# One branch over the general path, and layer two's first adjacency pieces loaded inside layer one

## The chip, the cores and the metric

The kernel runs on one core of one Trainium2 chip. The metric is the device time of one execution in microseconds (us); before the change the median of three runs is 2069.12 us.

## What is computed

Two graph convolutions on 6,250 nodes of 256 numbers, then a feed-forward layer that sends every node to two of eight experts:

```python
x = x + gnn(layernorm(x))      # two layers: relu(A_norm @ (h @ W) + b)
x = x + ffn(layernorm(x))      # top 2 of 8 experts, gelu(x @ W1 + b1) @ W2 + b2

def _gcn_conv(x, W, b, src, dst, n):
    h = x @ W
    deg = segment_sum(1, dst_with_loops);  dinv = rsqrt(deg)
    msgs = h[src] * (dinv[src] * dinv[dst])[:, None]
    return segment_sum(msgs, dst, num_segments=n) + b
```

There are 206,250 edges, sorted by destination. The lines of the two convolutions are shortened here; the layer norm has no weights of its own in front of the graph layers.

## The kernel before, in words

Nodes stand in 49 blocks of 128. The adjacency is held as counts: for a block of 128 destinations a tile `[128, 49 * 128]` of fp16 says how many edges lead from every source to every destination. A block's sum is then 49 matmuls of 128 x 512 (the node rows are kept as a high and a low fp16 half, hence 512 columns). For 40 of the 49 blocks the sums are made so ("dense"); for the other nine, source rows are gathered from DRAM ("takes", an indirect DMA on GpSimd, POOL, each followed by one matmul with a one-hot), 311 takes in a layer.

The program is a row of blocks (`nc.Block`), one after the other. In a block each of the five engines (TensorE PE, VectorE DVE, ScalarE ACT, GpSimd POOL, SyncE SP) has its own straight list of instructions; engines wait for each other by semaphores. At the end of a block all engines meet at a barrier, POOL clears the block's semaphores (L168) and all meet again (L169).

- **Layer one** (`build_layer_one`) builds the counts from one-hots `oh_lane` and `oh_cell` (VectorE, L802) by matmuls of one-hots (L954), empties them from PSUM (ScalarE, L1055), adds the self loops, sums (L925), takes (L567, L938) and writes to DRAM: each dense block's counts to `adj` for layer two (SP, L511), and each block's finished rows to `rows_d[1]` (SP, L514). A counter `n` over 512 banks and some steps after them sets the order of everything. At its end SP waits for the stores of the counts.
- **The general path** follows: four program blocks, `build_general_tables`, `build_general_rows`, `build_general_adjacency` and `build_general_layer`. They redo layer one for inputs that don't fit its tables. Whether the input fits stands in one word `fits`, set in layer one (L725). Each engine reads it once into a register (L305), and in each of the four blocks every engine compares it (`choose`, L307) and jumps over its own part. On this input all of them are jumped over. In the adjacency block a small index table (L1420, L1422, L1440) is computed in either case.
- **Layer two** (`build_layer_two`) reads `adj` back in half blocks ("pieces", 800 and 768 KB) into a ring of three (`ADJ_RING`), issued by SP (L1841), and sums again (L1871), with takes (L1798, L1887). A sum of a block is cut in five parts; part by part a slot counter orders what each engine does. Behind each sum follow the turn-over (`turn_over`), the product with the layer's weights `w` (`product`, L1905), and the rest on VectorE and ScalarE. SP first loads `w` and `b` (L1820, L1821), then three pieces, two blocks of `x` and small tables. PE and VectorE wait for `w` and `b` (`w_in`) before they begin. POOL writes rows of zeros to DRAM (L1768, L1769), starts a weight load, and takes from then on.
- **Routing and experts** come after it and are not touched.

All SBUF tiles have addresses: `rows[1]` is at the top of SBUF (`k.top`), the rest is allocated from below.

Of the kernel before, what the change touches and what calls it, by code (L numbers as in the profile page):

```python
# [193 lines left out]
def build_constants(k):  # L194

    nc = k.nc
    k.ident = k.sb("ident", [P, P], fp32)
    k.ones = k.sb("ones", [P, P], fp32)
    k.held_pool = k.sb("held_pool", [1, POOL_HOLDS + 1], fp32)
    k.held_act = k.sb("held_act", [P, 1], fp32)  # L200
    k.self_loop = k.sb("self_loop", [P, P], fp16)
    k.held_dve = k.sb("held_dve", [1, 1], fp32)
    k.eps = k.sb("eps", [P, 1], fp32)
    k.tri = k.sb("tri", [P, P], fp32)
# [12 lines left out]
    k.value_base = k.sb("value_base", [P, VALUES, TOKEN_TILES], fp32)  # L217
    k.pad_value = k.sb("pad_value", [P, 1], fp32)
    k.gb = k.sb("gb", [P, 2, EXPERTS * KF], fp32)
    k.b1 = k.sb("b1", [P, EXPERTS * HB], fp32)  # L220
    k.slot_gate = k.sb("slot_gate", [P, TOKEN_TILES], fp32)
    k.slot_token = k.sb("slot_token", [P, TOKEN_TILES], i32)
    k.pair_expert = k.sb("pair_expert", [1, 2 + PAIRS], i32)
    k.take_src = k.sb("take_src", [P, len(TAKES)], i32)
    k.take_lane = k.sb("take_lane", [P, len(TAKES), 2], bf16)
    k.ident_h = k.sb("ident_h", [P, P], fp16)
    k.rows_d = [k.dr(f"rows_d{n}", [PAD_NODES, 2 * D], fp16) for n in range(2)]
    k.rows1_out = k.nc.alloc_semaphore("rows1_out")
    k.adj = k.dr("adj", [BLOCKS, P, BLOCKS * P], fp16)
# [18 lines left out]
PLACE = {b: i for i, b in enumerate(ENDED)}  # L248

# [65 lines left out]
def build_layer_one(k, gst):  # L315
# [13 lines left out]
    k.fits = own("fits", [1, 1], u16)  # L329
# [3 lines left out]
    with ExitStack() as st:  # L333
# [57 lines left out]
        oh_lane = sb("m_oh_lane", [P, SLOTS_R, P], fp16)  # L391
        oh_cell = sb("m_oh_cell", [P, SLOTS_R, CELLS2], fp16)
# [21 lines left out]
        assert nc.sbuf_base <= k.top, nc.sbuf_base - k.top  # L414
# [69 lines left out]
        def _(sp):  # L484
# [597 lines left out]
def build_general_tables(k, gst):  # L1082
# [9 lines left out]
    with ExitStack() as st:  # L1092
# [50 lines left out]
        def _(sp):  # L1143
# [12 lines left out]
            choose(k, nc.sync, apart=apart)  # L1156

        @block.vector
        def _(dve):
# [107 lines left out]
            choose(k, nc.vector, apart=apart)  # L1267

        @block.scalar
        def _(act):  # L1270
# [17 lines left out]
            choose(k, nc.scalar, apart=apart)  # L1288

        @block.gpsimd  # L1290
        def _(pool):
# [16 lines left out]
            choose(k, nc.gpsimd, apart=apart)  # L1308

        @block.tensor  # L1310
        def _(pe):
# [27 lines left out]
            choose(k, nc.tensor, apart=apart)  # L1339


def build_general_rows(k):
# [3 lines left out]
    with ExitStack() as st:  # L1346
# [7 lines left out]
        @block.sync  # L1354
        def _(sp):
            def apart():
                sp.dma_start(xs[:], k.io["x"].rearrange("(b p) d -> p b d", p=P)).then_inc(x_in, 16)
            choose(k, nc.sync, apart=apart)

        @block.vector  # L1360
        def _(dve):
# [21 lines left out]
            choose(k, nc.vector, apart=apart)  # L1383

        @block.scalar
        def _(act):
            def apart():
                act.wait_ge(var_ready, BLOCKS)
                nc.scalar.activation(rstd[:], mv[:, :, 1], ACT.Sqrt, bias=k.eps[:]).then_inc(root, 1)
            choose(k, nc.scalar, apart=apart)  # L1390


def build_general_adjacency(k):
# [7 lines left out]
    with ExitStack() as st:  # L1401
# [17 lines left out]
        def _(pool):  # L1419
# [15 lines left out]
            choose(k, nc.gpsimd, apart=apart)  # L1435

        @block.vector
        def _(dve):
# [21 lines left out]
            choose(k, nc.vector, apart=apart)  # L1460

        @block.tensor
        def _(pe):
# [21 lines left out]
            choose(k, nc.tensor, apart=apart)  # L1485

        @block.scalar
        def _(act):
# [29 lines left out]
            choose(k, nc.scalar, apart=apart)  # L1518

        @block.sync  # L1520
        def _(sp):
# [8 lines left out]
            choose(k, nc.sync, apart=apart)  # L1530


def build_general_layer(k):
# [9 lines left out]
    with ExitStack() as st:  # L1543
# [20 lines left out]
        def _(sp):  # L1564
# [8 lines left out]
            choose(k, nc.sync, apart=body)  # L1573

        @block.tensor
        def _(pe):
# [38 lines left out]
            choose(k, nc.tensor, apart=body)  # L1615

        @block.scalar
        def _(act):
# [12 lines left out]
            choose(k, nc.scalar, apart=body)  # L1631

        @block.vector
        def _(dve):
# [24 lines left out]
            choose(k, nc.vector, apart=body)  # L1659


def build_layer_two(k):
# [4 lines left out]
    with ExitStack() as st:  # L1667
# [7 lines left out]
        adj = sb("_adj", [P, ADJ_RING, ADJ_HALF * P], fp16)  # L1675
# [29 lines left out]
        assert nc.sbuf_base <= k.top, nc.sbuf_base - k.top  # L1705
# [14 lines left out]
        adj_in = [sem(f"_adj_in{q}") for q in range(ADJ_RING)]  # L1720
# [98 lines left out]
        def _(sp):  # L1819
# [13 lines left out]
            def load_adj(o, m):  # L1833

                b, a = m // 2, m % 2 * ADJ_HALF
                n = min(ADJ_HALF, BLOCKS - a)
# [4 lines left out]
                sp.dma_start(adj[:, m % ADJ_RING, 0:n * P], k.adj[b][:, a * P:(a + n) * P]).then_inc(adj_in[m % ADJ_RING], 16)  # L1841

            def program(o):
# [9 lines left out]
                for slot in range(o.end):  # L1853
                    for m in range(2 * o.dense):
                        if slot == max(PARTS * (m - ADJ_RING + 1) // 2, 0):
                            load_adj(o, m)
# [6 lines left out]
        def _(pe):  # L1863
# [66 lines left out]
            pe.wait_ge(w_in, WEIGHTS)  # L1930
# [57 lines left out]
        def _(dve):  # L1988
# [112 lines left out]
            def program(o):  # L2101
# [44 lines left out]
            dve.wait_ge(w_in, WEIGHTS)  # L2146
# [469 lines left out]
```

## Time and profile before

| what | us |
|---|---|
| median of three runs | 2069.12 |
| fastest and slowest run | 2066.21, 2073.44 |
| span of the profiled execution (its own time from first to last instruction) | 2052.8 |
| what lies around the span, by the median | 16.3 |
| PE busy, share of the span | 1871.5, 91% |
| VectorE, GpSimd, ScalarE busy | 1351.6, 1143.9, 733.3 |

The page also cuts the span into 40 slices of 51.3 us; in tenths, PE's busy share and its granted clock are

```profile
PE   5789999999999975999999999944999999999997
PEclk9999999999999997999999999975999999999998
```

The profiled execution has no time of its own beside the span; the three runs were timed without a profile. Times in the rows below are counted from the start of the span. An engine's sequencer work (branches, barriers, loads of registers, issues of DMAs) is not counted as busy; in rows its engine has a "q" at the end, and PE's stands under "PEldq". "[9.60 <-X]" behind a row is the idle time of the engine before it and what ended it.

### The profile page before, as it was taken

To read this page: it belongs to the slowest core of one execution; us is meant where nothing else is said; L and a number is where in the kernel's file an instruction comes from. 1 tells how busy PE (TensorE), PEld (TensorE's weight loads), DVE (VectorE), ACT (ScalarE), POOL (GpSimd) and SP (SyncE) were. 2 spreads that over 40 slices of the span, in tenths; PEclk is the share of its full clock that TensorE was granted. 3 is DMA by queue.
4 is the path that set the end of the run, shared out by engine and by line. 5 is a ranking of instruction groups with operands and counts; after the bars stand their busy time and mean duration, and the time that the engine had idled before them with its cause. 6 is when DMAs were issued, how large, how long until landed. Compare 5 with 4: busy or idle time off the path is not lost. (4 is left out here: it accounts for less than half of the span.)

```text
span 2052.8 us, 40739 instructions
## 1 busy us (share of the span) xinstructions
PE 1871.5 (91%) x13425; PEld 1223.2 (60%) x13426; DVE 1351.6 (66%) x3358; ACT 733.3 (36%) x1669; POOL 1143.9 (56%) x1210
## 2 busy tenths in 40 slices
PE   5789999999999975999999999944999999999997
PEld 4545555554555532544544444423989989989996
DVE  7866766676667642566675757567676676666664
ACT  5744544444444420111111111112444444444442
POOL 6236666666666614667666666302455655555553
PEclk9999999999999997999999999975999999999998
DMA  9464555554455536787877788824233332333322
GB/s 292 121 217 167 180 191 173 174 181 167 170 181 174 177 121 215 242 278 259 266 249 270 268 303 269 283 83 193 42 50 52 49 49 47 49 49 49 50 44 27
DMA packets 126419, 329.51 MB, mean 161 GB/s; under 512 B 20736, under 2 KB 80000, under 8 KB 119360
## 3 DMA queue, kind: packets, MB, share of 16 engines
q0 software_dynamic: 59072, 142.05, 26.3%
q1 hardware_dynamic: 47376, 167.36, 22.7%
q10 hardware_dynamic: 19824, 18.23, 2.8%
q8 instruction: 82, 1.34, 0.3%
q14 instruction: 65, 0.53, 0.1%
HBM read 214.10 MB, written 113.45 MB: 160 GB/s over the span
## 5 line engine op out<-in xcount | busy, mean ns | idle before, releaser
L925 PE MATMUL mp_o<-rows,m_counts 128*128 128x512 f16 x1960 | 491.0, 382 | 8.5 <-ACT m_counts L1055 8.5
L1871 PE MATMUL rp_o<-rows,r_adj 128*128 128x512 f16 x1960 | 460.2, 382 | 31.3 <-DMA r_adj<-adj 31.3
L567 POOL DMA_INDIRECT m_x_t<-rows_d,take_src x311 | 368.2, 1184 | 202.6 <-PE mp_x L938 162.8
L1798 POOL DMA_INDIRECT r_took<-rows_d,take_src x311 | 323.7, 1041 | 186.4 <-PE rp_g L1887 122.1
L1055 ACT ACTIVATE m_counts<-mp 128x490 f16<-128x490 f32 (+4 forms) x544 | 292.2, 558 | 352.4 <-PE mp L954 346.0
L1871 PEld LDWEIGHTS rp_o<-rows,r_adj 128*128 128x128 f16 x1960 | 192.8, 98 | 251.0 <-DMA r_adj<-adj 31.8
L2427 PE MATMUL fp_h<-f_xt,w 128*128 128x256 f16 x2688 | 304.8, 274 | 0.3 <-DVE f_xt L2523 0.3
L2446 PE MATMUL fp_y<-w,f_hh 128*128 x2688 | 302.4, 273 | 0.0
L925 PEld LDWEIGHTS mp_o<-rows,m_counts 128*128 128x128 f16 x1960 | 183.0, 98 | 185.1 <-issue 11.5
L2427 PEld LDWEIGHTS fp_h<-f_xt,w 128*128 x2688 | 264.0, 98 | 31.7 <-issue 0.7
L2446 PEld LDWEIGHTS fp_y<-w,f_hh 128*128 128x128 f16 x2688 | 263.0, 98 | 30.4
L954 PEld LDWEIGHTS mp<-m_oh_cell,m_oh_lane 128*128 128x128 f16 x2560 | 163.8, 98 | 140.6 <-DVE m_oh_lane L802 24.8
L954 PE MATMUL mp<-m_oh_cell,m_oh_lane 128*128 128x98 f16 x2560 | 194.2, 208 | 29.7 <-DVE m_oh_lane L802 14.5
L2499 ACT ACTIVATE f_h<-fp_h,b 128x256 f32<-128x256 f32 x448 | 188.4, 475 | 76.1 <-PE fp_h L2427 71.4
L802 DVE TENSOR_TENSOR m_oh_lane<-lane_b,m_edge_lane 128x1920 f16<-128x1920 bf16 x171 | 201.8, 1180 | 8.9 <-PE mp L954 8.7
L2363 POOL DMA_INDIRECT out_dram<-f_weighted,f_to x112 | 184.8, 1650 | 30.4 <-issue 29.5
L180 POOL TENSOR_TENSOR held_pool<-held_pool 1x1 f32<-1x1 f32 x204 | 68.7, 339 | 210.7 <-DMA out_dram<-f_weighted,f_to 165.9
L2556 DVE TENSOR_TENSOR f_hh<-f_h,f_hh 128x512 f16<-128x512 f32 x224 | 156.1, 697 | 7.7
L802 DVE TENSOR_TENSOR m_oh_cell<-m_cells,m_edge_cell 128x1470 f16<-128x1470 bf16 x171 | 159.2, 931 | 0.0
L783 DVE TENSOR_TENSOR m_take_oh<-lane_b,take_lane 128x640 f16<-128x640 bf16 (+1 forms) x63 | 31.2, 496 | 191.4 <-PE mp_x L938 191.4
L2351 POOL DMA_INDIRECT f_xg<-xn_rows,f_stage x112 | 115.0, 1027 | 33.9 <-issue 33.4
L2532 DVE SCALAR_TENSOR_TENSOR f_y<-fp_y,b 128x256 f32<-128x256 f32 x112 | 47.4, 424 | 121.5 <-PE fp_y L2446 120.1
(260 smaller groups left out, 1877.2 us busy)
## 6 DMA issues: line engine op xcount, KB each, us to landing
adj<-m_counts SPq DMA_DIRECT2D x40, 1568.0 KB, 5.9
r_adj<-adj SPq DMA_DIRECT2D x40, 800.0 KB, 5.2
r_adj<-adj SPq DMA_DIRECT2D x40, 768.0 KB, 5.2
r_raw<-in_L_ffn_W_dram POOLq DMA_DIRECT2D x16, 1024.0 KB, 8.4
w_parts<-r_parts POOLq DMA_DIRECT2D x8, 1024.0 KB, 6.7
w<-w_parts SPq DMA_DIRECT2D x4, 2048.0 KB
rows<-in_x_dram SPq DMA_DIRECT2D x7, 896.0 KB, 20.1
rows_d<-rows SPq DMA_DIRECT2D x7, 896.0 KB, 4.6
```

Source lines behind the costliest of these rows:

```text
L567: pool.indirect_dma_start(out=took[:, r, :], out_offset=None, in_=k.rows_d[0], in_offset=bass.IndirectOffsetOnAxis(ap=k.take_src[:, i:i + ...
L802: nc.vector.tensor_tensor(out[:, r:r + items].rearrange("p r (v t) -> p r v t", t=2), bc(row[:].rearrange("p (v t) -> p v t", t=2)[:, None ...
L925: mm = nc.tensor.matmul(ps_o[q], counts[:, q, s, :], k.rows[0][:, s, :], start=i == 0, stop=i == BLOCKS - 1)
L954: mm = nc.tensor.matmul(bank(n)[:, i * CELLS2:(i + 1) * CELLS2], oh_lane[:, slot(n) + i, :], oh_cell[:, slot(n) + i, :], start=True, stop= ...
L1055: last = nc.scalar.activation(counts[:, q, :, lo - b * P:hi - b * P].rearrange("p h (a d) -> p h a d", d=STEP), items[:, :, (lo - first_ds ...
L1798: pool.indirect_dma_start(out=took[:, r, :], out_offset=None, in_=k.rows_d[1], in_offset=bass.IndirectOffsetOnAxis(ap=k.take_src[:, i:i + ...
L1871: mm = nc.tensor.matmul(ps_o[b % 2], adj[:, m % ADJ_RING, at:at + P], rows[:, s, :], start=s == 0, stop=s == BLOCKS - 1)
L2363: pool.indirect_dma_start(out=k.io["out"], out_offset=bass.IndirectOffsetOnAxis(ap=to[:, i:i + 1], axis=0), in_=weighted[:, i % YR, :], in ...
L2427: mm = nc.tensor.matmul(ps_h[b][:, j * PAIR:(j + 1) * PAIR], w, xt[:, q, xh, c, :], start=i == 0, stop=i == 5)
L2446: mm = nc.tensor.matmul(ps_y[s][:], hh[:, q, xh, h, s * P:(s + 1) * P], w, start=i == 0, stop=i == 3 * HB - 1)
L2499: g = nc.scalar.activation(h32[:, h, :], ps_h[b][:, j * PAIR:(j + 1) * PAIR], ACT.Gelu, bias=k.b1[:, bass.ds(ex[m + 1] * HB + h, 1)], scal ...
L2556: nc.vector.tensor_tensor(hh[:, q, 1, part], h32[:, part], hh[:, q, 0, part], ALU.subtract).then_inc(h_lo, 1)
```

## The change

Two edits, and what they need.

1. The four blocks of the general path are put under one branch: after layer one every engine loads the word `fits` again and compares it once (`nc.If`); the `choose` in each of the blocks goes. The word moves to the constants, so that it stays.
2. SP loads the first three adjacency pieces of layer two in layer one, at step 512, once the last bank of counts is made. The ring is a fixed piece of SBUF at the upper end of the one-hots `oh_lane` and `oh_cell`, which nobody reads after the last bank; their address is fixed for it. The semaphores of the ring, `adj_in`, live through both layers. Layer two's SP leaves out these three loads (`next_adj`). PE waits for `w_in` ahead of its first product, and VectorE ahead of its first `activate`, no longer at the beginning.

```diff
+    k.adj_in = [k.nc.alloc_semaphore(f"adj_in{q}") for q in range(ADJ_RING)]
+    k.oh_at = (k.top - SLOTS_R * (P + CELLS2) * 2) // 64 * 64
+    k.ring_at = (k.top - ADJ_RING * ADJ_HALF * P * 2) // 64 * 64
+    k.adj_ring = nc.alloc_sbuf_tensor_at("adj_ring", [P, ADJ_RING, ADJ_HALF * P], fp16, offset=k.ring_at)
...
+def load_adj(k, eng, m):
+
+    b, a = m // 2, m % 2 * ADJ_HALF
+    n = min(ADJ_HALF, BLOCKS - a)
+    eng.dma_start(k.adj_ring[:, m % ADJ_RING, 0:n * P], k.adj[b][:, a * P:(a + n) * P]).then_inc(k.adj_in[m % ADJ_RING], 16)
...
-        oh_lane = sb("m_oh_lane", [P, SLOTS_R, P], fp16)
-        oh_cell = sb("m_oh_cell", [P, SLOTS_R, CELLS2], fp16)
+        oh_lane = nc.alloc_sbuf_tensor_at("m_oh_lane", [P, SLOTS_R, P], fp16, offset=k.oh_at)
+        oh_cell = nc.alloc_sbuf_tensor_at("m_oh_cell", [P, SLOTS_R, CELLS2], fp16, offset=k.oh_at + SLOTS_R * P * 2)
...
                             sp.dma_start(k.adj[b], counts[:, b % 2].rearrange("p h d -> p (h d)")).then_inc(stored[b % 2], 16)
+                    if n == BANKS_D:
+
+                        sp.wait_ge(bank_done, BANKS_D)
+                        sp.wait_ge(stored[0], 16)
+                        sp.wait_ge(stored[1], 16)
+                        for m in range(ADJ_RING):
+                            load_adj(k, sp, m)
...
-            choose(k, nc.sync, apart=apart)
+            apart()
...
+                if m < ADJ_RING and o.takes:
+                    return
...
                 pe.wait_ge(agg_copied, b + 1)
                 if b:
                     pe.wait_ge(pre_ready, b)
+                else:
+                    pe.wait_ge(w_in, WEIGHTS)
...
-            pe.wait_ge(w_in, WEIGHTS)
             choose_order(nc.tensor, program)
...
                     q = i % 2
+                    if i == 0:
+                        dve.wait_ge(w_in, WEIGHTS)
...
-            dve.wait_ge(w_in, WEIGHTS)
             choose_order(nc.vector, program)
...
-            with ExitStack() as ust:
-                build_general_tables(k, ust)
-                build_general_rows(k)
-                build_general_adjacency(k)
-            build_general_layer(k)
+            flag = nc.alloc_registers("fits_all")
+            nc.regs_load(flag, k.fits[0:1, 0:1])
+            with nc.If(nc.snap(flag, min_val=0, max_val=1) < 1):
+                with ExitStack() as ust:
+                    build_general_tables(k, ust)
+                    build_general_rows(k)
+                    build_general_adjacency(k)
+                build_general_layer(k)
```

Where `choose` went, the same change stands fourteen more times; it is shown once. How the instructions of an engine's list move is shown at three places. A name in brackets is the semaphore an instruction waits for; semaphores are used again, so a wait of layer two stands under the name that its number had first in layer one. `rows_49` and `rows_50` are `rows[1]`.

**PE, from the last sum of layer one to the end of the first jump.** Before (the last two rows belong to the first of the four blocks, whose entry is the row with the barrier):

```order
L925 MATMUL mp_o<-rows,m_counts 128x512 [waits m_emptied,m_agg]
L925 MATMUL mp_o<-rows,m_counts 128x512 x47
L925 MATMUL mp_o<-rows,m_counts 128x512 [waits m_looped]
L307 UNCONDITIONAL_BRANCH
L1310 UNCONDITIONAL_BRANCH [waits barrier_Pool_Activation_PE_DVE_SP_release]
L307 COMPARE_AND_BRANCH
L307 UNCONDITIONAL_BRANCH
```

Now:

```order
L943 MATMUL mp_o<-rows,m_counts 128x512 [waits m_emptied,m_agg]
L943 MATMUL mp_o<-rows,m_counts 128x512 x47
L943 MATMUL mp_o<-rows,m_counts 128x512 [waits m_looped]
L319 UNCONDITIONAL_BRANCH
L2592 TENSOR_LOAD fits [waits barrier_Pool_Activation_PE_DVE_SP_release]
L1775 COMPARE_AND_BRANCH
L1328 UNCONDITIONAL_BRANCH
```

The wait for the barrier has the flag's load behind it in place of the entry to the first block, and one comparison; the rows of the blocks that follow have no comparison of their own.

**PE, the beginning of layer two.** `m_io` is the wait for `w` and `b`; `m_hi`, `m_lo` and `m_cells` are the three pieces. Before:

```order
L1602 MATMUL sp_h<-s_w,s_agg_t 128x256
L310 UNCONDITIONAL_BRANCH
L1862 UNCONDITIONAL_BRANCH [waits barrier_Pool_Activation_PE_DVE_SP_release]
L307 COMPARE_AND_BRANCH [waits m_io]
L1871 MATMUL rp_o<-rows_49,r_adj 128x512 [waits m_hi]
L1871 MATMUL rp_o<-rows_49,r_adj 128x512 x24
L1871 MATMUL rp_o<-rows_49,r_adj 128x512 [waits m_lo]
L1871 MATMUL rp_o<-rows_49,r_adj 128x512 x23
```

Now:

```order
L1775 UNCONDITIONAL_BRANCH [waits barrier_Pool_Activation_PE_DVE_SP_release]
L1880 UNCONDITIONAL_BRANCH
L319 COMPARE_AND_BRANCH
L1889 MATMUL rp_o<-rows_50,adj_ring 128x512 [waits adj_in0]
L1889 MATMUL rp_o<-rows_50,adj_ring 128x512 x24
L1889 MATMUL rp_o<-rows_50,adj_ring 128x512 [waits adj_in1]
L1889 MATMUL rp_o<-rows_50,adj_ring 128x512 x23
L1889 MATMUL rp_o<-rows_50,adj_ring 128x512 [waits adj_in2]
```

The comparison no longer waits for the weights, and the pieces' semaphores are those that layer one's SP raises; the wait `m_io` stands at the first `rp_h<-r_w,r_agg_t`, behind the first takes.

**SP, the end of layer one.** `m_lo2` is a finished row block. Before:

```order
L511 DMA adj<-m_counts 128x6272 [waits m_looped]
L514 DMA rows_d<-rows_49 128x512 [waits m_lo2]
L511 DMA adj<-m_counts 128x6272 [waits m_looped] x2
L514 DMA rows_d<-rows_49 128x512 [waits m_lo2] x5
L307 UNCONDITIONAL_BRANCH [waits m_rows0_out,m_stored1,m_stored0]
L1142 UNCONDITIONAL_BRANCH [waits barrier_Pool_Activation_PE_DVE_SP_release]
L307 COMPARE_AND_BRANCH
```

Now:

```order
L532 DMA rows_d<-rows_50 128x512 [waits m_lo2]
L522 DMA adj<-m_counts 128x6272 [waits m_looped] x2
L260 DMA adj_ring<-adj 128x3200 [waits m_stored1,m_stored0,m_bank]
L260 DMA adj_ring<-adj 128x3072
L260 DMA adj_ring<-adj 128x3200
L532 DMA rows_d<-rows_50 128x512 [waits m_lo2] x5
L319 UNCONDITIONAL_BRANCH [waits m_rows0_out,m_stored1,m_stored0]
L2592 TENSOR_LOAD fits [waits barrier_Pool_Activation_PE_DVE_SP_release]
L1775 COMPARE_AND_BRANCH
```

Three loads of pieces stand between the last two stores of counts and the last five writes of rows; the three `r_adj<-adj` in front of `r_x<-in_x_dram` in layer two are gone from SP's list.

## Rows read from the trace of the kernel before

**Rows 1.** The page, part 1, whole span: busy us, share, instructions.

```profile
PE 1871.5 (91%) x13425; PEld 1223.2 (60%) x13426; DVE 1351.6 (66%) x3358; ACT 733.3 (36%) x1669; POOL 1143.9 (56%) x1210
```

**Rows 2.** Page, part 5: group, count | busy us, mean ns | idle before.

```profile
L1871 PE MATMUL rp_o<-rows,r_adj 128*128 128x512 f16 x1960 | 460.2, 382 | 31.3 <-DMA r_adj<-adj 31.3
```

**Rows 3.** Timeline, 735 to 800 us: start, duration, what [idle before].

```profile
748.53 10.74 PE L925 MATMUL mp_o<-rows,m_counts 128*128 128x512 f16 x49 [0.76 <-ACT m_counts L1055]
749.30 12.65 SPq L514 DMA_DIRECT2D rows_d<-rows  x5
760.62 0.99 DVE L762 TENSOR_TENSOR rows<-m_act_in,rows 128x256 f16<-128x256 f32 x2
781.81 0.40 SPq L1820 DMA_DIRECT2D r_w<-in_L_gnn_W_dram  x1
783.34 1.33 SPq L1841 DMA_DIRECT2D r_adj<-adj  x3
790.62 9.75 PE L1871 MATMUL rp_o<-rows,r_adj 128*128 128x512 f16 x33 [31.34 <-DMA r_adj<-adj]
```

**Rows 4.** PE's release from a block's barrier (L169), first and fifth.

```profile
L169 PEldq EVENT_SEMAPHORE  x1: 51/51/51, 763.4 to 763.4; - x1
...
L169 PEldq EVENT_SEMAPHORE  x1: 51/51/51, 781.7 to 781.7; - x1
```

**Rows 5.** PE's branches (L307) in three blocks: min/median/max ns, starts.

```profile
L307 PEldq COMPARE_BRANCH  x2: 73/1737/3401, 763.6 to 763.7; - x2
...
L307 PEldq COMPARE_BRANCH  x2: 71/1920/3770, 772.0 to 772.1; - x2
...
L307 PEldq COMPARE_BRANCH  x2: 77/1918/3758, 776.9 to 777.0; - x2
```

**Rows 6.** PE in layer one: flag's load (L305), branch falling through (L307).

```profile
L305 PEldq TENSOR_LOAD <-fits x1: 479/479/479, 75.6 to 75.6; - x1
...
L307 PEldq COMPARE_BRANCH  x1: 88/88/88, 76.2 to 76.2; - x1
```

**Rows 7.** First and fourth block: branches, and the first instruction (DRAIN) behind.

```profile
L307 POOLq COMPARE_BRANCH  x2: 39/40/41, 763.5 to 763.5; - x2
...
L1092 POOLq DRAIN  x1: 115/115/115, 764.0 to 764.0; - x1
...
L307 DVEq COMPARE_BRANCH  x2: 43/45/47, 776.8 to 776.9; - x2
...
L1543 DVEq DRAIN  x1: 59/59/59, 781.0 to 781.0; - x1
```

**Rows 8.** Stretches: us, busy us of five engines, clock, DMA share, GB/s.

```profile
749.00:755.00 6.00, 6.00 (x29) 2.71 (x28) 0.71 (x3) 0.42 (x1) 0.00 (x0) 1.00 0.84 333
763.00:782.00 19.00, 0.00 (x0) 0.00 (x0) 0.70 (x3) 0.00 (x0) 1.18 (x3) 0.50 0.04 11
...
761.50:790.60 29.10, 0.00 (x0) 0.00 (x0) 2.69 (x11) 0.00 (x0) 3.91 (x10) 0.50 0.27 88
790.60:795.60 5.00, 4.99 (x12) 1.79 (x13) 0.00 (x0) 0.00 (x0) 2.82 (x3) 0.50 1.02 416
795.60:800.60 5.00, 5.00 (x24) 2.25 (x23) 0.00 (x0) 0.00 (x0) 3.79 (x5) 1.00 1.04 378
```

**Rows 9.** DMA issues: KB each, us to landing; one load, 40 stores (L511).

```profile
r_b<-in_L_gnn_b_dram SPq DMA_DIRECT2D x1, 128.0 KB, 6.4
...
adj<-m_counts SPq DMA_DIRECT2D x40, 1568.0 KB, 5.9
```

**Rows 10.** Layer two's first takes: issue, PE's use (timeline), landing (DMA list).

```profile
792.17 1.04 POOL L1798 DMA_INDIRECT r_took<-rows_d,take_src  x1 [7.44 <-DMA xn_rows<-r_took]
...
805.60 0.59 PE L1887 MATMUL rp_g<-r_took,r_take_oh 128*128 128x512 f16 x2
...
r_took<-rows_d,take_src POOLq DMA_INDIRECT x8, 6.4
```

**Rows 11.** Waits of POOL, 790 to 1360 us: total us, times, longest.

```profile
POOL r_took L1798 <- PE rp_g L1887: 122.1, 130, 4.3
```

More of the change, by code:

```diff
@@ L203, in build_constants @@
     k.eps = k.sb("eps", [P, 1], fp32)
+    k.fits = k.sb("fits", [1, 1], u16)
     k.tri = k.sb("tri", [P, P], fp32)
@@ L328, in build_layer_one @@
     own = lambda name, shape, dt: gst.enter_context(nc.sbuf_tensor(name, shape, dt))
-    k.fits = own("fits", [1, 1], u16)
     k.fits_flag = {}
@@ L413, in build_layer_one @@
         took = x_t[:].rearrange("p r c n -> p (r c n)").bitcast(fp16).rearrange("p (r d) -> p r d", r=TAKE_RING)
-        assert nc.sbuf_base <= k.top, nc.sbuf_base - k.top
+        assert nc.sbuf_base <= k.oh_at, nc.sbuf_base - k.oh_at
         ps = st.enter_context(nc.psum_tensor("mp", [P, BANKS * BANK], fp32))
@@ L1266, in apart @@
                 nc.vector.memset(k.edge_cell[:, ITEMS:], -1.0)
-            choose(k, nc.vector, apart=apart)
+            apart()
         @block.scalar
@@ L1287, in apart @@
                 nc.scalar.activation(tot[:], tmp[:], ACT.Sqrt).then_inc(root_done, 1)
-            choose(k, nc.scalar, apart=apart)
+            apart()
         @block.gpsimd
@@ L1307, in apart @@
                             in_offset=bass.IndirectOffsetOnAxis(ap=tile_i[:, c:c + 1], axis=0)).then_inc(got[c % 4], 16)
-            choose(k, nc.gpsimd, apart=apart)
+            apart()
         @block.tensor
@@ L1338, in apart @@
                         nc.tensor.transpose(ps_t[(2 * c + j) % 4][:], rows[:, c % 4, :], k.ident[:]).then_inc(t_done, 1)
-            choose(k, nc.tensor, apart=apart)
+            apart()
 def build_general_rows(k):
@@ L1357, in apart @@
                 sp.dma_start(xs[:], k.io["x"].rearrange("(b p) d -> p b d", p=P)).then_inc(x_in, 16)
-            choose(k, nc.sync, apart=apart)
+            apart()
         @block.vector
@@ L1382, in apart @@
                     link(nc.vector.tensor_tensor(lo, xs[:, b, :], hi, ALU.subtract))
-            choose(k, nc.vector, apart=apart)
+            apart()
         @block.scalar
@@ L1389, in apart @@
                 nc.scalar.activation(rstd[:], mv[:, :, 1], ACT.Sqrt, bias=k.eps[:]).then_inc(root, 1)
-            choose(k, nc.scalar, apart=apart)
+            apart()
 def build_general_adjacency(k):
@@ L1434, in apart @@
                 in_pairs(nc.gpsimd, BLOCKS, loop)
-            choose(k, nc.gpsimd, apart=apart)
+            apart()
         @block.vector
@@ L1459, in apart @@
                 in_pairs(nc.vector, BLOCKS, one_hots)
-            choose(k, nc.vector, apart=apart)
+            apart()
         @block.tensor
@@ L1484, in apart @@
                 in_pairs(nc.tensor, BLOCKS, items)
-            choose(k, nc.tensor, apart=apart)
+            apart()
         @block.scalar
@@ L1517, in apart @@
                 in_pairs(nc.scalar, BLOCKS, empty)
-            choose(k, nc.scalar, apart=apart)
+            apart()
         @block.sync
@@ L1529, in apart @@
                     sp.wait_ge(stored[q], 16 * ((BLOCKS + 1 - q) // 2))
-            choose(k, nc.sync, apart=apart)
+            apart()
 def build_general_layer(k):
@@ L1572, in body @@
                     sp.dma_start(adj[:, q, :], k.adj[b]).then_inc(adj_in[q], 16)
-            choose(k, nc.sync, apart=body)
+            body()
         @block.tensor
@@ L1614, in body @@
                             product(b - 1)
-            choose(k, nc.tensor, apart=body)
+            body()
         @block.scalar
@@ L1630, in body @@
                     nc.scalar.activation(k.rows[1][:, b, 0:D], pre[:, q, :], ACT.Copy).then_inc(hi_done, 1)
-            choose(k, nc.scalar, apart=body)
+            body()
         @block.vector
@@ L1658, in body @@
                                             ALU.subtract).then_inc(lo_done, 1)
-            choose(k, nc.vector, apart=body)
+            body()
 def build_layer_two(k):
@@ L1674, in build_layer_two @@
         brow = sb("_b", [P, D], fp32)
-        adj = sb("_adj", [P, ADJ_RING, ADJ_HALF * P], fp16)
+        adj = k.adj_ring
         took = sb("_took", [P, TAKE_RING, 2 * D], fp16)
@@ L1704, in build_layer_two @@
         dense = sb("_dense", [P, BLOCKS, EXPERTS], fp32)
-        assert nc.sbuf_base <= k.top, nc.sbuf_base - k.top
+        assert nc.sbuf_base <= k.ring_at, nc.sbuf_base - k.ring_at
         ps_o = [pb(f"p_o{i}", [P, 2 * D], fp32) for i in range(2)]
@@ L1719, in build_layer_two @@
                                     "gates_out"))
-        adj_in = [sem(f"_adj_in{q}") for q in range(ADJ_RING)]
+        adj_in = k.adj_in
         took_in = [sem(f"_took_in{r}") for r in range(TAKE_RING)]
@@ L1831, in small, with next_adj @@
                 sp.dma_start(b1_rows, k.io["L0_ffn_b1"].rearrange("e (c p) -> (e c) p", p=P)).then_inc(small_in, 16)
-            def load_adj(o, m):
-                b, a = m // 2, m % 2 * ADJ_HALF
-                n = min(ADJ_HALF, BLOCKS - a)
+            def next_adj(o, m):
+                if m < ADJ_RING and o.takes:
+                    return
                 if m >= ADJ_RING and (m - ADJ_RING) % 2 == 0:
@@ L1840, in load_adj @@
                     sp.wait_ge(summed, o.place[(m - ADJ_RING) // 2] + 1)
-                sp.dma_start(adj[:, m % ADJ_RING, 0:n * P], k.adj[b][:, a * P:(a + n) * P]).then_inc(adj_in[m % ADJ_RING], 16)
+                load_adj(k, sp, m)
             def program(o):
@@ L1855, in program @@
                         if slot == max(PARTS * (m - ADJ_RING + 1) // 2, 0):
-                            load_adj(o, m)
+                            next_adj(o, m)
                     for i in range(BLOCKS):
```

## The prediction

> **What bounds the kernel now.** I read the page's engine shares first: TensorE (PE) is busy for 91% of the span [rows 1], so time is won mostly where it stands still. The costliest groups of instructions come next. The 1,960 adjacency matmuls of layer two (L1871) have 31.3 us of idle time in front of them, all of it put down to the load `r_adj<-adj`, and none besides [rows 2]: inside layer two the sums run back to back. The timeline shows the stop itself: the last matmul of layer one ends at 748.53 + 10.74 = 759.3 us, the first of layer two starts at 790.6 [rows 3]. The page's releaser names only the wait that ended last, so I split the stop. From 759.3 to 763.4 layer one ends: VectorE finishes the last row block (760.62 + 0.99 = 761.6), SP issues its write (749.30 + 12.65 = 761.95), then the barriers at the end of the block [rows 3, 4]. From 763.4 to 781.7, 18.3 us, five engines pass four program blocks of the general path, in which on this input nothing but an index table is computed [rows 4]. From 781.7 to 790.6, 8.9 us, PE waits for its first loads: they are issued at 781.81 (weights) and 783.34 (adjacency), and the matmul starts at 790.62 [rows 3].
>
> Why are empty blocks dear? The branch rows answer. PE's second branch in three of the blocks lasts 3.40, 3.77 and 3.76 us, although a branch that just falls through lasts 0.09 [rows 5, 6]; so I read a jump over a long skipped body as a wait for the code at its target. VectorE shows the same as a late arrival: branch at 776.9, next instruction at 781.0. POOL, whose skipped body in the first block is short, arrives at 764.0 after a branch at 763.5 [rows 7]. Every block then adds its barriers, and its slowest jump is paid again.
>
> **The change, part by part.**
>
> *One branch for four blocks.* The barrier release at 763.4 stays. What follows is one load of the flag, one comparison and one jump. Load to branch takes 0.6 us on PE where layer one does the same (75.6 to 76.2) [rows 6]. The new jump, over all the bodies at once, is not in the trace. Nearest rows: PE's three jumps, 3.40 to 3.77 [rows 5], and VectorE's 4.1 [rows 7]. Lower end: no wait at all, 0.1, if the target happened to be there. Upper end: two such waits in a row, 4.1 + 3.8 = 7.9, if the first piece of code ends soon after the target or the five engines' fetches hinder each other. I take 3.8, PE's own dearer row. PE then stands at layer two's first branch at 763.4 + 0.1 + 0.6 + 3.8 = 767.9, instead of 781.7.
>
> *The first three pieces loaded ahead.* SP now issues them behind the 40th adjacency store and ahead of the last five row writes: three issues, 1.33 us [rows 3]. Three of the row writes are ready at once and go 1.3 us later, nobody being in need of them; the last are ready only near 761, so SP has the time. Bytes: store 1,568 KB, pieces 800 + 768 + 800 KB, three row writes of 128 KB, 4.4 MB. The engines moved 333 GB/s in 749 to 755 and 416 GB/s when the same pieces were loaded in layer two [rows 8], so the burst that begins at 748.9 is over between 759.5 and 762.2. The pieces are there 6 us before PE wants them. Layer one's end waits for the 40th store: by the median of all 40 it lands 5.9 us after its issue [rows 9], at 754.8, and even last in the burst by 762.2 against an end at 762.0. I take 0; the ends are 0 and 0.2.
>
> *Waits for the weights moved to the first product.* PE no longer waits for `w` and `b` ahead of the sums, VectorE not ahead of its first one-hots. `r_b` lands 6.4 us after its issue [rows 9]; with SP in layer two by 768.3 at the latest and 1.4 us for both issues that is 776.1 at the latest. PE's first product stands behind the first take, 805.60 - 790.62 = 15.0 us after the start [rows 3, 10], so at 783 or later. Nothing waits; if the cover were gone, PE would stand with the sums queued behind it.
>
> With both gone PE starts about 0.3 us (my choice; a branch of 0.09 and the first issue) after it arrives, at 768.2: **22.4 us earlier** than 790.6. Ends of the unknown jump: 764.5 (26.1 earlier) and 772.3 (18.3 earlier).
>
> *What is late next.* POOL's first take. Before, it is issued at 792.17, 10.5 us after POOL entered layer two, of which 7.44 are a wait for a zero row to land among the adjacency loads; takes then land after 6.4 us [rows 10]. If POOL enters no earlier than PE (767.9) and nothing gets quicker, take 0 lands at 784.8, and PE wants it at 768.2 + 15.0 = 783.2: a stall of 1.6. If POOL arrives early, as its short jump lets me expect, or the zero row no longer shares the engines with 2.4 MB of pieces, none. I take 0.
>
> *Clock.* PE's granted clock is 0.50 from 761.5 to 795.6, the lower level (1.2 GHz), though PE worked until 759.3; the first 12 matmuls of layer two take 5.0 us, the next 24 as long at 1.00 [rows 8]. Restarting at 768.2 still comes after a stop of 8.9 us, so I count the same slow start on both sides: 0. Ends: 2.5 us won if the clock is up (12 matmuls at full rate), 2.5 lost if the low stretch doubles.
>
> *Nothing for the rest.* One-hots and tiles at other addresses, the flag among the constants, semaphores held outside the blocks: the same instructions with the same shapes, no row shows a price, and I bound it by 0 on both sides. The rest of the program starts 22.4 us earlier and runs as before: in layer two POOL waits for PE 130 times, 122.1 us in all [rows 11], so PE sets that stage and the shift is carried through.
>
> Sum: span 2052.8 - 22.4 = 2030.4. What lies around the span is 2069.12 - 2052.8 = 16.3 us by the median of the runs, and stays. **2046.7 us**, 1.1% below that median.
>
> **Rivals.**
>
> *A. The jump is dearer.* Five engines fetch at once, and the transfers that fetch code may meet data. For it: three of four blocks show 3.4 us or more with few engines fetching; these fetches ran while the engines moved 11 GB/s [rows 8], the kindest case. Against it: by my burst the ring is in by 762.2. Price: about one more wait, 3.8: 2050.5 us. The Trainium skill, "DMA: Bandwidth & Descriptors", section "Issuing engines are not separate DMA queues", says that transfers issued by any engine run on the same 16 DMA engines and interleave; it speaks against loads placed shortly before a jump. The trace has no jump beside a busy queue, so it neither confirms nor denies it for code.
>
> *B. The takes gate the start.* The stall of 1.6 above, up to 4 with slower landings: 2048.3 to 2050.7. For: two transfers stand between POOL's entry and PE's need. Against: fewer bytes at that moment.
>
> *C. The other way: slower.* The code of layer two no longer arrives in time. Before, the engines stood 8.9 us at its door after their jump, time for later code to be brought in; now they run on at once, and PE could wait again and again along its stream. Place: gaps between L1871's successors with no releaser. Price 3.4 to 3.8 each; from seven of them on (7 x 3.4 = 23.8) the change loses, and ten cost 38 - 22.4 = 15.6: 2084.7 us. Against: nothing but the load wait stands before those 1,960 matmuls now [rows 2], so the stream keeps up once it runs.
>
> *D. Hardly anything changes.* The burst delays the store on which layer one's end waits, or the branch isn't reached earlier, so that 16 of the 22 us go. It would need the store at 778, against the 762.2 of the worst sharing: 2063 to 2069 us.
>
> *E. A cheaper start.* The jump finds its target, or the clock is up: 2041 to 2044.5 us.
>
> **How the numbers follow.** Forecast 0.62, A 0.17, B 0.08, E 0.07, C 0.03, D 0.03. About 0.3%, 6.2 us, can be told from no change, as the runs of before spread from 2066.21 to 2073.44. Forecast, A, B and E are all faster by more: 0.94; D is the same: 0.03; C slower: 0.03. The range takes in A with its upper end (2050.8) and E (2041), widened by some 3 us at the top and 1 at the bottom for that spread: 2040 to 2054.
>
> **What would show it.** Right: PE's idle time in front of the first adjacency matmul of layer two near 9 us instead of 31.3; one branch row of 3.4 to 4 us on PE near 764; no releaser `adj_ring<-adj` for that wait; the three loads issued near 750 and landed by 762; the distance from that matmul to the end as before. Wrong in the jump: the branch row at 7 us, or a gap without a releaser soon after the start. Wrong in the takes: PE waiting for `r_took` some 15 us after its start. Wrong altogether: layer one ending later than 763.4, or idle time spread along layer two.

## The result, and the profile after

The change takes 2046.77 us, the median of four runs (2043.71 to 2052.19); before takes 2069.31, the median of four (2066.21 to 2073.44). The ratio is 0.988 with a 95% interval of 0.9861 to 0.9899: faster by 1.2% (the medians alone differ by 22.5 us, 1.1%). The forecast was 2046.7.

The profiled execution of the change has a span of 2045.8 us and a time of 2047.49. Its page has this for the costliest matmuls of layer two (columns as in [rows 2]):

```profile
L1889 PE MATMUL rp_o<-rows,adj_ring 128*128 128x512 f16 x1960 | 455.9, 380 | 8.9 <-issue 8.9
```

31.3 us of idle time have become 8.9, and the releaser is no load any more. The timeline of 760 to 802 us shows the boundary (columns as in [rows 3]):

```profile
766.41 10.74 PE L943 MATMUL mp_o<-rows,m_counts 128*128 128x512 f16 x49 [0.76 <-ACT m_counts L1073]
...
767.27 2.59 SPq L260 DMA_DIRECT2D adj_ring<-adj  x3
769.90 9.94 SPq L532 DMA_DIRECT2D rows_d<-rows  x5
...
778.50 0.99 DVE L780 TENSOR_TENSOR rows<-m_act_in,rows 128x256 f16<-128x256 f32 x2
...
782.22 0.39 SPq L1838 DMA_DIRECT2D r_w<-in_L_gnn_W_dram  x1
...
786.04 14.06 PE L1889 MATMUL rp_o<-rows,adj_ring 128*128 128x512 f16 x58 [8.89 <-issue]
...
788.00 1.04 POOL L1816 DMA_INDIRECT r_took<-rows_d,take_src  x1 [3.05 <-DMA xn_rows<-r_took]
...
799.93 0.59 PE L1905 MATMUL rp_g<-r_took,r_take_oh 128*128 128x512 f16 x2
```

Layer one's last matmul ends at 766.41 + 10.74 = 777.15 us, layer two's first starts at 786.04. SP issues the three pieces at 767.27, right at the start of that last block of matmuls, as forecast. The take that PE needs first is issued at 788.00 and used at 799.93; POOL waits 3.05 us for its zero row, where it waited 7.44 [rows 10], and PE has no idle time at 799.93. What is left of the stop shows in the sequencers' rows (columns as in [rows 4]):

```profile
L169 PEldq EVENT_SEMAPHORE  x1: 51/51/51, 781.3 to 781.3; - x1
...
L2592 PEldq TENSOR_LOAD <-fits x1: 298/298/298, 781.5 to 781.5; - x1
...
L1775 SPq COMPARE_BRANCH  x1: 50/50/50, 781.7 to 781.7; - x1
...
L1775 PEldq COMPARE_BRANCH  x1: 3912/3912/3912, 781.9 to 781.9; - x1
```

The barrier lets PE go at 781.3, as long after the last matmul (4.2 us) as before (4.1). Load and comparison of the flag take 0.6 us to 781.9, the one jump 3.91, and 0.2 us later PE is at work. SP's branch lasts 0.05 us: its next instruction, the load of the weights, goes at 782.22, beside PE's jump. The windows (columns as in [rows 8]) show the burst of the ring, and the clock at the restart:

```profile
766.80:780.80 14.00, 10.35 (x48) 4.49 (x46) 2.88 (x8) 0.91 (x3) 0.00 (x0) 1.00 0.92 335
781.00:782.00 1.00, 0.00 (x0) 0.00 (x0) 0.00 (x0) 0.00 (x0) 0.00 (x0) 1.00 0.00 0
782.00:788.80 6.80, 2.76 (x7) 1.04 (x8) 1.74 (x9) 0.00 (x0) 3.50 (x9) 0.50 0.71 188
788.80:793.80 5.00, 5.00 (x24) 2.25 (x23) 0.00 (x0) 0.00 (x0) 3.79 (x5) 1.00 0.99 356
```

The burst from 766.8 runs for 14.0 us at 335 GB/s and is over just before the jump: from 781 to 782 us nothing moves. The granted clock is still 1.00 in that row; it is 0.50, the lower level of 1.2 GHz, from 782.0 to 788.8 only, and 1.00 behind it; before it was 0.50 from 761.5 to 795.6 [rows 8].

**A surprise in the sum.** The two profiled spans, 2052.8 and 2045.8 us, differ by 7.0 us, the medians by 22.5. The rest lies at the beginning. In the stretch from 34 to 56 us the first profile of before has (same columns)

```profile
34.00:56.00 22.00, 17.98 (x88) 13.62 (x87) 20.13 (x50) 13.45 (x37) 16.22 (x16) 0.92 1.04 334
```

and the profile of the change

```profile
34.00:56.00 22.00, 5.95 (x14) 3.72 (x15) 10.16 (x22) 1.54 (x4) 14.43 (x14) 0.59 0.86 264
```

so PE is busy there for a third of the time it was (14 matmuls recorded, against 88), and everything behind is some 18 us late: the last block of layer one starts at 766.41 where it started at 748.53 [rows 3]. The first experiment asks whose delay that is.

### The profile page after: what moved, and what is told of

It reads as the page before. It is cut to its first block and busy times, and to the rows that moved or that the text cites. A ratio compares the mean times of both kernels' runs of the same rounds, so it can differ in the third digit from the quotient of the medians.

```text
span 2045.8 us, 40624 instructions
## 1 busy us (share of the span) xinstructions
PE 1867.4 (91%) x13425; PEld 1222.5 (60%) x13426; DVE 1345.9 (66%) x3357; ACT 729.1 (36%) x1669; POOL 1146.3 (56%) x1208
## 5 line engine op out<-in xcount | busy, mean ns | idle before, releaser
L1889 PE MATMUL rp_o<-rows,adj_ring 128*128 128x512 f16 x1960 | 455.9, 380 | 8.9 <-issue 8.9
L1889 PEld LDWEIGHTS rp_o<-rows,adj_ring 128*128 128x128 f16 x1960 | 191.9, 98 | 225.9 <-issue 11.2
L2383 POOL DMA_INDIRECT out_dram<-f_weighted,f_to x112 | 190.2, 1699 | 30.2 <-issue 29.1
L2519 ACT ACTIVATE f_h<-fp_h,b 128x256 f32<-128x256 f32 x448 | 183.2, 481 | 66.1 <-PE fp_h L2447 62.3
L2495 ACT ACTIVATE held_act<-ones 128x1 f32<-128x1 f32 x56 | 11.4, 203 | 316.2 <-PE fp_x L2431 301.8
```

The costliest lines, as they stand in the source:

```text
L1889: mm = nc.tensor.matmul(ps_o[b % 2], adj[:, m % ADJ_RING, at:at + P], rows[:, s, :], start=s == 0, stop=s == BLOCKS - 1)
L2383: pool.indirect_dma_start(out=k.io["out"], out_offset=bass.IndirectOffsetOnAxis(ap=to[:, i:i + 1], axis=0), in_=weighted[:, i % YR, :], in ...
L2519: g = nc.scalar.activation(h32[:, h, :], ps_h[b][:, j * PAIR:(j + 1) * PAIR], ACT.Gelu, bias=k.b1[:, bass.ds(ex[m + 1] * HB + h, 1)], scal ...
```

## The experiments

"Stop" is the idle time that the timeline gives in front of layer two's first adjacency matmul.

| run | stop, us | PE's jump, us | median of runs, us |
|---|---|---|---|
| before, first profile | 31.34 | 3.40, 3.77, 3.76 | 2069.31 |
| before again | 32.03 | 3.76, 4.03, 3.84 | 2068.78 |
| branch only | 16.09 | 4.21 | 2052.23 |
| loads only | 22.16 | 3.42, 3.27, 3.46 | 2062.06 |
| weights waited for at the front | 9.82 | 3.91 | 2047.13 |
| the change | 8.89 | 3.91 | 2046.77 |
| one more block | 13.92 | 3.31, 4.49 | 2054.39 |
| three pieces by the jump | 12.97 | 6.68 | 2049.44 |
| two pieces by the jump | 11.42 | 5.63 | 2049.28 |
| one piece by the jump | 9.16 | 3.84 | 2047.55 |
| x loaded one piece after the other | 8.49 | 3.52 | 2046.32 |

Runs of one kernel spread over up to 14 us, so a few us are read from the stop, not from the median.

### Before, once more

No edit.

> The kernel before, unchanged. Question: the profiled execution of before has a span of 2052.8 us, 16.3 below the median of its timed runs, while every run of the change lies only 1.7 us above its own span; and the first 100 us of the change's profile are some 18 us longer than those of before's. Theory (a lucky profile): the first profile of before caught an execution with a quick beginning; typical runs of before begin as slowly as the change does. Then the span here is 1.7 us below the time, 2064 to 2071, the last matmul block of layer one starts near 766 (748.5 in the first profile), and the stop from its end to the first adjacency matmul of layer two is again 31 us. Rival (the change slows the beginning): the span is again near 2053 beside a time of 2054.5 to 2069, layer one's last block starts near 749, and the moved tiles or the constants cost the change 18 us at its beginning that some other gain pays for.

Measured: 2068.78 us, ratio to before 0.9998 (0.9984 to 1.0012), span 2067.1, 1.7 below that execution's time of 2068.78. Its window from 34 to 56 us is that of the change:

```profile
34.00:56.00 22.00, 5.70 (x13) 3.52 (x14) 13.50 (x34) 1.92 (x5) 13.54 (x14) 0.60 0.85 272
```

The flag that ends the tables of layer one is loaded by PE at 75.6 us in the first profile of before [rows 6], here (same columns) at

```profile
L305 PEldq TENSOR_LOAD <-fits x1: 476/476/476, 93.5 to 93.5; - x1
```

and in the change at

```profile
L317 PEldq TENSOR_LOAD <-fits x1: 474/474/474, 94.1 to 94.1; - x1
```

The stop is what it was:

```profile
808.93 6.29 PE L1871 MATMUL rp_o<-rows,r_adj 128*128 128x512 f16 x19 [32.03 <-DMA r_adj<-adj]
```

So the first profile of before shows an untypically quick execution, and the slow beginning is no cost of the change. Of the 51 times of before in all the comparisons made here, none is below 2064 us. The two profiles of before also differ in how much they recorded: the first holds 26,872 updates of semaphores, the second 17,664. Whether the first execution was quick by chance, or because it was recorded in another way, no run shows.

### The branch alone

```diff
-                    if n == BANKS_D:
-                        sp.wait_ge(bank_done, BANKS_D)
...
-                            load_adj(k, sp, m)
...
-                if m < ADJ_RING and o.takes:
-                    return
...
+            pe.wait_ge(w_in, WEIGHTS)
             choose_order(nc.tensor, program)
...
+            dve.wait_ge(w_in, WEIGHTS)
             choose_order(nc.vector, program)
```

> The change without its loads: one branch over the general path, but the three pieces are loaded at the front of layer two and PE and VectorE wait for the weights there, as before. Theory (jump and loads overlap): SP's jump is short, so its loads go out some 2.4 us after the barrier release and land 7.3 us later, beside PE's jump; PE starts 4.9 us later than with the whole change, the stop is 9.3 + 4.9 = 14.2 us, the gain 31.3 - 14.2 = 17.1: 2052.2 us. Rival (additive, as the prediction summed): the gain is 18.3 - 4.5 = 13.8 and the load wait of 8.9 stays whole behind the jump: stop 17.5, 2055.5 us. Rival (the branch does nothing by itself): 2069 us.

Measured: 2052.23 us, ratio 0.9923 (0.9902 to 0.9944). PE's jump (columns as in [rows 5]), and the timeline:

```profile
L1768 PEldq COMPARE_BRANCH  x1: 4213/4213/4213, 778.6 to 778.6; - x1
```

```profile
780.20 2.52 SPq L260 DMA_DIRECT2D adj_ring<-adj  x3
...
789.88 14.28 PE L1880 MATMUL rp_o<-rows,adj_ring 128*128 128x512 f16 x58 [16.09 <-DMA adj_ring<-adj]
```

SP's loads go out at 780.20, while PE jumps from 778.6 to 782.8, so part of their time is covered. But the first piece comes 9.7 us after its issue, where it took 7.3 before (783.34 to 790.62 [rows 3]). Why it took longer is not shown. The stop of 16.09 stands between the two theories (14.2 and 17.5): some of the load wait is covered, but less than the first had it. The median agrees with the first (2052.2), yet the interval of the ratio takes in both, so the time alone could not have told them apart. The rival that the branch does nothing by itself is out.

### The loads alone

Each of the four blocks has its own comparisons again, in place of the one branch:

```diff
-            apart()
+            choose(k, nc.tensor, apart=apart)
```

> The change without its branch: the four blocks each keep their own comparison, the pieces are loaded inside layer one and the waits for the weights stand at the first product. Theory: the 18.3 us from the barrier to layer two's branch stay, only the 8.9 us of load wait go down to about 0.3: stop 22.7 us, gain 8.6, 2060.7 us. By both theories of overlap the same here; with the branch alone at 17.1 the two gains add to 25.7 against 22.4 for both, 3.3 us counted twice; with 13.8 they add to 22.4. Rival (the code of layer two must be fetched after the jump, so part of the load wait was never the loads'): PE waits 3 to 4 us without a releaser where the loads stood, gain 5, 2064 us.

Measured: 2062.06 us, ratio 0.9957 (0.9941 to 0.9974).

```profile
800.82 14.17 PE L1889 MATMUL rp_o<-rows,adj_ring 128*128 128x512 f16 x58 [22.16 <-PEq L169]
```

The stop falls by 9.2 us against the first profile and 9.9 against the second: the load wait goes whole, and no wait for code stands where it was. PE's release from the last barrier is at 800.5, its first matmul at 800.82. That rival is out. Branch (15.3 to 15.9 us) and loads (9.2 to 9.9) add to 24.4 to 25.8, both together bring 22.5 to 23.1: some 2 to 3 us are in both, the part of the loads that lies beside the jump.

### The waits for the weights at the front

```diff
-                else:
-                    pe.wait_ge(w_in, WEIGHTS)
...
+            pe.wait_ge(w_in, WEIGHTS)
             choose_order(nc.tensor, program)
```

and the same on VectorE.

> The change with the waits for the weights back at the front of layer two, on PE and VectorE; branch and loads as in the change. Theory: SP issues the weights 0.9 us after the barrier release, the bias 0.7 later lands after 6.4 us, so PE may start 8.0 us after the release, against 4.7 in the change: stop 12.6 us, 3.3 us later than the change, 2050.1 us. Rival (the weights land in time behind the jump): 2046.8, stop 9.3. Rival (the moved waits matter more, since VectorE's one-hots for the takes are late as well): PE also stands ahead of its first take, 2052 us or more.

Measured: 2047.13 us, ratio 0.9898 (0.9871 to 0.9925).

```profile
786.87 14.00 PE L1889 MATMUL rp_o<-rows,adj_ring 128*128 128x512 f16 x58 [9.82 <-DMA r_b<-in_L_gnn_b_dram]
```

My 3.3 us were too many: the bias, issued at 782.56, is there when PE's wait ends at 786.7, 4.2 us after the issue and not 6.4 [rows 9]. No pieces are loaded beside it now, which may be the reason; no run tests it. The wait that was moved costs 0.9 us where it stood, too little to see in the time. The rival by which it costs nothing comes nearest.

### One more block

The last block of the general path stands outside the branch again, with comparisons of its own:

```diff
-                build_general_layer(k)
+            build_general_layer(k)
```

> The change with the last of the four blocks of the general path taken out from under the branch again: it keeps its own comparisons, its jump over its body and its barriers. Everything else as in the change. Theory (each block costs a jump and its barriers, whatever stands before it): in the profile of before that block takes 4.9 us from release to release, so the stop grows from 9.3 to 14.2 us and the time from 2046.8 to 2051.7 us; PE shows two long branches, each 3.3 to 4.2 us. Rival (a second jump is cheap, since the first has already brought code in): only the barriers, about 1.1 us, come on top: stop 10.4, 2047.9 us. Rival (the time of a jump grows with the code jumped over): the first is shorter and the second also, the two together about 3.9 plus 1.1: 2047.9 us as well, but with two branch rows of about 2 us each.

Measured: 2054.39 us, ratio 0.9928 (0.9907 to 0.995). PE's two jumps, and the stop:

```profile
L1581 PEldq COMPARE_BRANCH  x1: 3313/3313/3313, 781.5 to 781.5; - x1
...
L319 PEldq COMPARE_BRANCH  x2: 73/2280/4488, 784.9 to 785.1; - x2
```

```profile
790.70 15.21 PE L1889 MATMUL rp_o<-rows,adj_ring 128*128 128x512 f16 x58 [13.92 <-PEq L169]
```

The stop grows by 5.0 us, as the first theory has it (4.9). A second jump is not cheaper for the first, and neither is shorter for having less to skip: 3.31 us over three blocks, 4.49 over one. The median is 2.7 us above the expected 2051.7 and all four runs lie above it; the four runs of the change alone spread over 8.5 us, so these 2.7 us stay unsettled.

### The loads beside the jump

```diff
-                    if n == BANKS_D:
...
-                            load_adj(k, sp, m)
...
                 sp.wait_ge(rows0_out, 16 * X_LOADS)
+                for m in range(ADJ_RING):
+                    load_adj(k, sp, m)
```

> The change with the three loads of pieces moved from behind the last bank of counts to the very end of SP's list of layer one, behind its last waits, so that 2.4 MB are in flight while PE jumps. Theory (data hardly hurts a jump; the late loads hurt by themselves): SP's three issues delay the end of layer one by about 1.3 us; PE's jump stays at 3.9 to 4.2; the first piece lands some 8.5 us after its issue at 780.0, so PE restarts near 788.5 instead of 786.0: 2049.3 us. Rival A of the prediction (code and data share the 16 engines, so the jump takes one wait more): branch row of 7 us or more, PE restarts near 790 or later: 2051 us or more. Rival (place of the loads doesn't matter, as they land beside barrier and jump): 2046.8 to 2048 us.

Measured: 2049.44 us, ratio 0.9895 (0.9872 to 0.9918). The time is the theory's; the way to it is nearly rival A's. Jump and timeline:

```profile
L1770 PEldq COMPARE_BRANCH  x1: 6676/6676/6676, 783.8 to 783.8; - x1
```

```profile
780.52 1.31 SPq L260 DMA_DIRECT2D adj_ring<-adj  x3
...
790.67 14.06 PE L1884 MATMUL rp_o<-rows,adj_ring 128*128 128x512 f16 x58 [12.97 <-issue]
```

The jump takes 6.68 us. The list of the DMA queues (packets, MB, share of the engines) says why. First 784 to 787 us, then 787 to 788:

```profile
q1 hardware_dynamic: 226, 1.21, 101.3%
...
q1 hardware_dynamic: 46, 0.29, 105.7%
q14 instruction: 4, 0.03, 10.2%
q8 instruction: 1, 0.02, 8.1%
```

For three microseconds behind the branch the 16 engines are full with data and no packet of instructions moves; then four packets of one queue and one of the other come, and PE goes on. In the change four such packets move at once, from 782 to 783 us:

```profile
q14 instruction: 4, 0.03, 11.8%
```

Two more runs vary what is in flight.

### One and two pieces beside the jump

```diff
-                        for m in range(ADJ_RING):
+                        for m in (0, 1):
                             load_adj(k, sp, m)
...
                 sp.wait_ge(rows0_out, 16 * X_LOADS)
+                for m in (2,):
+                    load_adj(k, sp, m)
```

and `(0,)` with `(1, 2)`.

> As the run with the loads beside the jump, but only the third piece (800 KB, wanted 21 us after the restart) is issued at the end of SP's list; the first two stay where the change has them. With three pieces there PE's jump lasted 6.68 us instead of 3.91, and the code it waits for began to move only at 787.1, when the data ahead of it had drained. Theory (code waits behind the data that is in flight, in proportion to its bytes): the barrier comes 0.4 us later, 0.8 MB drain in 2.3 us and are gone before the jump's fetch: branch row 3.9 to 4.3 us, stop 9.7 to 10.2, 2047.4 us. Rival (any large transfer begun near the jump costs it a whole second wait): 6.5 to 7 us, stop 12.4, 2050 us.

> As before with the second and third piece (1.57 MB) at the end of SP's list. Theory (in proportion to bytes in flight): the barrier comes 0.9 us later; the pieces, issued from 780.0 on, drain at some 320 to 400 GB/s by 784.0 to 785.0, about 1 us behind the moment of the fetch: branch row 4.2 to 5.3 us, stop 10.5 to 11.6, 2048.5 us. Rival (all or nothing): 6.5 to 7 us as with three, stop 12.9, 2050.5 us. Rival (the 6.68 us with three pieces was chance): 3.9 us.

Measured: 2047.55 us (ratio 0.9878, 0.9847 to 0.9909) and 2049.28 us (0.9896, 0.9865 to 0.9928). One piece:

```profile
L1777 PEldq COMPARE_BRANCH  x1: 3836/3836/3836, 782.4 to 782.4; - x1
```

```profile
780.09 0.36 SPq L260 DMA_DIRECT2D adj_ring<-adj  x1
...
786.45 15.49 PE L1891 MATMUL rp_o<-rows,adj_ring 128*128 128x512 f16 x58 [9.16 <-issue]
```

Two pieces:

```profile
L1777 PEldq COMPARE_BRANCH  x1: 5632/5632/5632, 780.7 to 780.7; - x1
```

```profile
777.88 0.85 SPq L260 DMA_DIRECT2D adj_ring<-adj  x2
...
786.50 14.88 PE L1891 MATMUL rp_o<-rows,adj_ring 128*128 128x512 f16 x58 [11.42 <-issue]
```

With 0, 0.8, 1.57 and 2.37 MB begun behind layer one's last row write the jump takes 3.91, 3.84, 5.63 and 6.68 us. These are one profile each, but the last two lie above every jump with no such load beside it (3.27 to 4.49 in the table), and the packets of instructions say why (the profile doesn't tell for which engine a packet is): the first one behind PE's branch starts at 782.7, 783.8, 783.4 and 787.1 us, that is 0.8, 1.4, 2.7 and 3.3 us after the branch. So it is neither chance nor all or nothing: the code waits behind the data that is still in flight. With 0.8 MB it comes 0.6 us later and the jump is no longer for it. With two pieces I had the upper end at 5.3. That branch only has 4.21, like a jump with nothing beside it, fits as well: its instruction packets start from 779.4 to 779.7 us, before SP issues the first piece at 780.20.

### The beginning

SP waits for each piece of `x` to land before it issues the next one.

```diff
+                if g >= 1:
+                    sp.wait_ge(x_in[g - 1], 16)
                 sp.dma_start(xs[:, g * n:(g + 1) * n, :],
```

> The change, with the loads of x at the beginning of layer one sent one after the other: SP waits for each piece of 896 KB to land before it issues the next, where it had up to six outstanding. This tests the beginning, not the change: in all profiles but the first one of before, updates of semaphores come 4 to 7 us late between about 33 and 57 us, while the engines move 350 GB/s, and layer one is some 18 us longer. Theory (too many transfers outstanding hold up the updates): with fewer the late updates go, layer one's flag is there near 76 instead of 94 us, and the time falls by up to 18 us, to 2029 us. Rival (the late updates have another cause): the flag stays near 94, 2047 us. Rival (the gating itself costs): the last pieces of x come later than they are needed, the flag is later than 94, 2050 us or more.

Measured: 2046.32 us, ratio 0.9885 (0.9861 to 0.991). PE loads the flag at 93.2 us, against 94.1 in the change and 75.6 in the quick execution. Neither 18 us won nor 3 lost: the number of loads of `x` outstanding is not what holds up the beginning.

## Why the prediction was right

**Confirmed, step by step.** The release 4.1 us after the last matmul: 4.2. Flag and comparison 0.6: 0.6. The jump 3.8, within 0.1 and 7.9: 3.91. The start at most 0.3 behind it: 0.2. From release to first matmul 4.8: 4.7. Stop shorter by 22.4: 22.45 (31.34 - 8.89). That one jump replaces three was the largest choice of the forecast, and "one more block" shows that it was the right price: 5.0 us for a block with its barriers.

**The ring.** The burst was to end between 10.6 and 13.3 us after its beginning; it took 14.0, a little longer than the worst that I had allowed, since all five row writes fell into it (4.69 MB) where I had counted three (4.4 MB). Layer one ended no later for it, so rival D did not come either. Had it taken two more it would have met the jump's code, and the three runs with pieces beside the jump show the price.

**The takes, the weights, the code behind the jump.** No stall at the first take, so rival B did not come. The weights' wait at the first product costs nothing: PE starts it at 805.55 us with no idle time before it. At the front the wait would cost 0.9. Rival C had PE starving for code along layer two: from its first adjacency matmul to the first matmul of the routing (1374.95) the change takes 588.9 us, before took 591.6 (790.62 to 1382.21) and 587.7 in the second profile, so nothing is lost there.

**Rival A** did not come in the change, but its mechanism is real: 6.68 us with three pieces in flight. The Trainium skill, "DMA: Bandwidth & Descriptors", section "Issuing engines are not separate DMA queues", says that transfers of all issuing engines interleave on the same 16 DMA engines; these runs extend that to the transfers of code. The Trainium skill's "Runtime: NRT & Kernel Launch", section "Instruction fetch mechanics", says that a taken branch out of the part at hand must fetch its target by DMA before the engine goes on; the instruction packets behind the branch agree.

**Clock.** I counted 0 within 2.5 either way. Seven matmuls run in the stretch at 0.50 where twelve did [rows 8], about 5 x 0.2 = 1 us won. Rival E lies there, at a small size. (Its times were added up a little wrong: by its own terms, 3.7 us for the jump and 2.5 for the clock, alone or together, it reaches from 2040.5 to 2044.2.)

**The step that failed** is the last: "What lies around the span is 2069.12 - 2052.8 = 16.3 us by the median of the runs, and stays." Around a span lie 1.7 us, in every run of the change and in before's second profile. The other 14.6 us were the difference between one quick execution and the usual ones. The forecast span of 2030.4 was therefore too low by 15.4, and the term of 16.3 too high by 14.6; they cancel, because taking the gain from the median comes to the same thing. Had I asked why a span should lie 16 us below the time, the right sum was at hand: median minus gain.

**Still open** is why the beginning is slow. In the change's profile and in before's second some updates of semaphores come 4 us and more after the instruction that makes them, from about 33 to 57 us, and few are recorded: between 18 and 56 us 868 in the quick execution, 121 in the change, 157 in before's second profile. The Trainium skill, "NOTIFIC — the notification-queue block", section "7.1 Overflow: three behaviours, one of which stalls the engine", says that the unit that writes such records has a mode in which it stalls the engine that makes them while its queue is full; whether that happens here no run shows. Both kernels have it alike, and one of the twelve runs of the loads alone, at 2050.93 us some 11 below their median, may have been spared it too.

## What to carry to other kernels

A skipped block is not free: on PE each far jump with no large load beside it took 3.3 to 4.5 us however much code it passed, with barriers about 5, so put one branch around all that is skipped together. Load what comes after the jump early enough to have landed, for code comes over the same DMA engines, and 2.4 MB in flight made the jump 2.8 us longer. And set a gain read from one profiled execution against the median of runs; where a span and its times differ by more than a few us, take a second profile before explaining the difference.

## What the runs showed that was not expected

Data delays a jump by what is still in flight: 3.91, 3.84, 5.63 and 6.68 us for 0, 0.8, 1.57 and 2.37 MB, and with 2.37 MB no instruction packet moved in the three microseconds from 784 to 787 us. And two executions of one kernel can differ by 14.3 us (spans of 2052.8 and 2067.1), with the whole difference made before the flag of layer one is loaded (75.6 and 93.5 us; 3.6 of these 17.9 us come back behind it).
